# Ten state buffers, an earlier GpSimd inflow, later products with D and earlier SiLU gates in a two-direction Mamba decoder layer

## The reference, cut to what matters

```python
xz = jnp.einsum('bld,ed->ble', x, Win)
u, z = jnp.split(xz, 2, axis=-1)
uc = _silu(causal_conv4(u))                    # 512 channels
x_dbl = jnp.einsum('bld,ed->ble', uc, Wx)      # 16 ranks, 32 B rows, 32 C rows
dt = softplus(x_dbl[..., :16] @ Wdt.T + bdt)
A = -exp(Alog)                                 # 512 channels x 32 states
h = exp(dt_t * A) * h + (dt_t * u_t) * B_t     # step over 100 tokens
y = einsum('bdn,bn->bd', h, C_t) + uc * Dp
y = y * _silu(z)
out = einsum('bld,ed->ble', y, Wout)
```

## Time and profile before

| | before |
|---|---|
| median of 3 runs | 1164.34 us (1163.25 to 1166.03) |
| profiled execution, its time | 1168.91 us |
| its span in the trace | 1166.8 us |
| PE busy | 1009.4 us (87%) |
| DVE busy | 808.7 us (69%) |
| ACT busy | 756.4 us (65%) |
| POOL busy | 628.8 us (54%) |
| granted TensorE clock, mean | 0.945 |

### The profile page before, as it was taken

How to read it: one execution, slowest core, us unless ns; L and a number is a source line. 1 busy time by engine, 2 the same in 40 slices (tenths; PEclk the granted TensorE clock), 3 DMA queues, 4 the chain that set the end, 5 groups by cost and what they waited for, 6 DMA issues and landing times.

```text
span 1166.8 us, 16801 instructions
## 1 busy us (share of the span) xinstructions
PE 1009.4 (87%) x5808; PEld 691.1 (59%) x5808; DVE 808.7 (69%) x954; ACT 756.4 (65%) x1727; POOL 628.8 (54%) x389
## 2 busy tenths in 40 slices
PE   5795788988889898888988898898989799799995
PEld 3342554555555455554555566677767556699994
DVE  6786999998999989999899945756666721111110
ACT  4789998888989888898888911455565532133331
POOL 2000899898999989899899933421210005022222
PEclk9897799999999999999999999979998979899998
DMA  5001333343444433343444401430000006689994
GB/s 180 8 7 36 87 108 108 98 109 91 116 110 96 117 96 103 107 106 105 102 109 106 107 22 62 131 93 15 14 2 2 2 0 220 216 257 321 300 319 113
DMA packets 91119, 125.45 MB, mean 108 GB/s; under 512 B 11641, under 2 KB 84490, under 8 KB 91018
## 3 DMA queue, kind: packets, MB, share of 16 engines
q1 hardware_dynamic: 87130, 120.04, 35.8%
q0 software_dynamic: 3904, 4.33, 2.0%
HBM read 115.93 MB, written 9.23 MB: 107 GB/s over the span
## 4 chain that ended last, share of the span: by engine, by line
PE 37%; DVE 26%; issue 12%; DMA 11%; POOL 6%; ACT 6%; DVEq 0%; POOLq 0%; ACTq 0%
DVE states L1681 14%; PE ps L1186 12%; DMA sums<-y_tile,x_tile 10%; DVE states L1659 5%; PE ps L1077 4%; PE ps L1067 3%; PE ps L1167 3%; POOL states L663 3%; PE ps L1279 3%; PE ps L1291 2%; POOL states L672 2%; PE ps L1084 2%; DVE neg_max L1762 2%; PE ps L1177 2%; ACT probs L989 2%
## 5 line engine op out<-in xcount | busy, mean ns | idle before, releaser
L672 POOL TENSOR_TENSOR states<-states,c_row 128x800 f32<-128x800 f32 x255 | 473.9, 1889 | 131.8 <-DVE states L1681 131.8
L1186 PE MATMUL ps<-states,ident 128*128 128x400 f32 x1024 | 370.7, 506 | 0.0
L1186 PEld LDWEIGHTS ps<-states,ident 128*128 128x128 f32 x1024 | 188.2, 193 | 119.2 <-issue 7.5
L1681 DVE TENSOR_TENSOR_SCAN states<-ps,states 128x800 f32<-128x800 f32 x128 | 230.5, 1801 | 12.4 <-POOL states L663 12.4
L1681 DVE TENSOR_TENSOR_SCAN states<-sb_decay,ps 128x800 f32<-128x800 f32 x128 | 231.4, 1808 | 10.7 <-ACT sb_decay L901 10.6
L893 ACT ACTIVATE xT<-xn_tok,xT 100x256 f32<-100x256 f32 x512 | 216.4, 493 | 14.8 <-PE ps L1167 14.7
L901 ACT ACTIVATE ps<-dt,neg_a 128x396 f32<-128x396 f32 x256 | 141.8, 586 | 57.9 <-DVE states L1681 56.9
L1167 PE MATMUL ps<-ident,xT 100*128 100x100 f32 x1024 | 113.9, 255 | 73.1 <-DVE states L1681 70.9
L1167 PEld LDWEIGHTS ps<-ident,xT 100*128 100x128 f32 x1024 | 97.9, 144 | 131.6 <-issue 127.0
L901 ACT ACTIVATE sb_decay<-dt,neg_a 128x396 f32<-128x396 f32 x256 | 144.4, 612 | 2.4 <-DVE states L1681 2.4
L1048 ACT ACTIVATE hid_tile<-ps,w_tile 128x128 f32<-128x128 f32 x160 | 45.6, 368 | 105.0 <-PE ps L1490 105.0
(11 more groups left out here) (225 smaller groups left out, 1270.1 us busy)
## 6 DMA issues: line engine op xcount, KB each, us to landing
c_row<-rows SPq DMA_DIRECT2D x256, 200.0 KB, 3.1
w_tile<-in_w SPq DMA_DIRECT2D x40, 1024.0 KB, 7.9
b_row<-rows SPq DMA_DIRECT2D x32, 200.0 KB, 3.1
ctx<-in_ctxT SPq DMA_DIRECT2D x8, 361.0 KB, 4.1
rows_by_slot<-blank_rows SPq DMA_DIRECT2D x1, 2660.0 KB, 11.5
x_tile<-rows_by_slot SPq DMA_DIRECT2D x20, 133.0 KB, 3.7
win<-in_winT SPq DMA_DIRECT2D x2, 1024.0 KB, 10.8
w_shared<-in_w SPq DMA_DIRECT2D x2, 1024.0 KB, 6.6
```

The costliest lines, as they stand in the source:

```text
L672: nc.gpsimd.tensor_tensor(st, st, c_row[i % C_SLOTS][:].unsqueeze(1).broadcast_to([P, CP, TQ]), ALU.mult).then_inc(product_ready, 1)
L1186: mm = nc.tensor.matmul(ps[:, j, 0:TQ], ident[:], states[i % RING][:, j * TQ:(j + 1) * TQ], start=False, stop=(i % N == N - 1), skip_group ...
L1681: nc.vector.tensor_tensor_scan(st, rates, inflows, 0.0, ALU.mult, ALU.add).then_inc(scan_done, 1)
```

## The change

What it does:

- `RING` goes from 8 to 10 state buffers (4 x 800 bytes per partition each).
- GpSimd issues `pool_inflow` three rounds ahead of its step (POOL_AHEAD) instead of two.
- The products with D no longer open a segment. The first `sum_state` of a segment starts the accumulation (and waits for `y_gated` there), and the products with D join it behind the sum of state 12 (`add_skip`, SKIP_AT = 12).
- On TensorE the row of B for the next VectorE inflow is issued in the round of the inflow before it (so the one of step 9 mod 8 moves from round 7 to round 5), and in a segment's start the transposes of step 8 are issued in round 6, ahead of the sum of state 1, instead of round 7.
- The z tiles of channels 0 and 1 of direction 0 are computed right behind `x` and go from PSUM through SiLU straight into `gate`, while SiLU's table is still in from the convolution; direction 0's `x` rows are copied ahead of the last two SiLUs of the convolution. The other z tiles come ahead of their dt tile. The SiLU of the other six gate tiles stands right behind the last dt tile, and the scaled tokens of step 2 stand behind the decays of step 1.

The diff, cut:

```diff
@@ -55,12 +55,12 @@
-RING = 8
+RING = 10
 SEG = DIRS * Q * (CT // CP)
 STEPS = SEG * N
 C_SLOTS, B_SLOTS = 4, 1
 POOL_EVERY, POOL_AT = 8, 7
-SUM_LAG, GATE_AT = 5, 5
+SUM_LAG, GATE_AT, SKIP_AT = 5, 5, 12
 TURNED_AT, TURN_EVERY = 0, 2
 TURN_DTU_AT, COPY_DTU_AT = (9, 15), (11, 17)
 SCALED_SLOTS, SB_DECAYS = 2, 2
@@ -130,6 +132,17 @@
 
 POOL_STEPS, DVE_STEPS, TURNED_STEPS = counts_of(on_pool), counts_of(on_dve), counts_of(turned_in)
 BANK_STEPS = [i + 1 - TURNED_STEPS[i] for i in range(STEPS)]
+
+
+def products_of(d):
+
+    early = [("z", c) for c in range(CT) if d == 0 and c < SILU_EARLY]
+    rest = []
+    for c in range(CT):
+        if ("z", c) not in early:
+            rest.append(("z", c))
+        rest.append(("dt", c))
+    return early + rest
 
 
 def bank_jobs():
@@ -150,9 +163,8 @@
     for d in range(DIRS):
         for q in range(Q):
             jobs.append((("x", d, q), "a"))
-        for c in range(CT):
-            channel("dt", d, c)
-            channel("z", d, c)
+        for name, c in products_of(d):
+            channel(name, d, c)
     for d in range(DIRS):
         for h in range(B // 2):
             jobs.append((("mix", d, h), "a"))
@@ -674,8 +687,8 @@
 
             pool.wait_ge(dtu_ready, DIRS * CT)
             for i in range(STEPS - 1):
-                if on_pool(i + 2) and i + 2 < STEPS:
-                    pool_inflow(i + 2)
+                if on_pool(i + POOL_AHEAD) and i + POOL_AHEAD < STEPS:
+                    pool_inflow(i + POOL_AHEAD)
                 state_times_c(i)
 
             last = STEPS - 1
@@ -849,21 +862,24 @@
                 steps += 2
                 nc.scalar.activation(dt_sb[d][:, c, :], e, ACT.Ln, bias=1.0).then_inc(log_ready, 1)
 
-            def copy_gates(d, c):
+            def copy_gates(d, c, func=ACT.Copy):
                 for q in range(Q):
-                    copy_out(("z", d, c, q), gate[d][:, c, chunk(q)], bank(("z", d, c, q))[:, 0:TQ])
-
-            def silu_gates(d):
-                job_copied(act, ("z", d, CT - 1, Q - 1))
-                for c in range(CT):
-                    nc.scalar.activation(gate[d][:, c, :], gate[d][:, c, :], ACT.Silu).then_inc(gate_ready, 1)
+                    copy_out(("z", d, c, q), gate[d][:, c, chunk(q)], bank(("z", d, c, q))[:, 0:TQ], func)
+
+            def silu_gates(d, c):
+                job_copied(act, ("z", d, c, Q - 1))
+                nc.scalar.activation(gate[d][:, c, :], gate[d][:, c, :], ACT.Silu).then_inc(gate_ready, 1)
 
             steps = 0
-            for g in range(DIRS * CT):
+            units = DIRS * CT
+            for g in range(units):
                 copy_u(*divmod(g, CT))
-                if g >= 1:
+                if 1 <= g < units - 1:
                     silu_u(*divmod(g - 1, CT))
-            silu_u(DIRS - 1, CT - 1)
+            copy_x(0)
+            for g in range(units - 2, units):
+                silu_u(*divmod(g, CT))
+                copy_gates(0, g - (units - SILU_EARLY), ACT.Silu)
             nc.scalar.preload_act_table_set("natural_log_exp_and_others")
 
             for d in range(DIRS):
@@ -871,10 +887,17 @@
                 nc.scalar.activation(neg_a[d][:], neg_a[d][:], ACT.Exp).then_inc(rate_ready, 1)
             act.wait_ge(conv_ready, DIRS * CT)
             for d in range(DIRS):
-                copy_x(d)
+                if d:
+                    copy_x(d)
+                for name, c in products_of(d):
+                    if name == "dt":
+                        softplus_parts(d, c)
+                    elif d or c >= SILU_EARLY:
+                        copy_gates(d, c)
+            for d in range(DIRS):
                 for c in range(CT):
-                    softplus_parts(d, c)
-                    copy_gates(d, c)
+                    if d or c >= SILU_EARLY:
+                        silu_gates(d, c)
 
             def copy_dtu(s, h, at=DTU_BANK):
                 act.wait_ge(dtu_turned, 2 * s + h + 1)
@@ -922,14 +945,12 @@
                 copy_dtu(0, h, FIRST_DTU_BANKS[h])
             act.wait_ge(b_tok_ready, 1)
             scale_tokens(0)
-            scale_tokens(2)
-            for d in range(DIRS):
-                silu_gates(d)
             act.wait_ge(neg_a_ready, DIRS)
             act.wait_ge(dt_ready, DIRS * CT)
             sb_decays(0)
             act.wait_ge(decay_zeroed, 1)
             bank_decays(1)
+            scale_tokens(2)
             sb_decays(2)
             for i in range(1, STEPS, 2):
                 if i > 1:
@@ -1111,15 +1132,17 @@
                 for q in range(Q):
                     product(("x", d, q), 2 * N + R, TQ, [
                         (wx_sb[d][:, c, :], u_sb[d][:, c, chunk(q)]) for c in range(CT)])
-                pe.wait_ge(rank_ready, Q * (d + 1))
-                for c in range(CT):
+                for name, c in products_of(d):
+                    if name == "z":
+                        in_product("z", 1, d, c)
+                        continue
+                    pe.wait_ge(rank_ready, Q * (d + 1))
                     for q in range(Q):
                         product(("dt", d, c, q), P, TQ, [(wdt_sb[d][:, tile(c)], rank_sb[:, chunk(q)])])
-                    in_product("z", 1, d, c)
 
 
             pe.wait_ge(consts, CONSTS)
-            for key, _ in JOBS[JOB[("z", DIRS - 1, CT - 1, Q - 1)] - 7:][:8]:
+            for key, _ in JOBS[LAST_OF_MIXER - 7:][:8]:
                 job_copied(pe, key)
             pe.wait_ge(parts_ready, DIRS)
             pe.wait_ge(diag_ready, DIRS)
@@ -1168,23 +1191,24 @@
                                                  scaled[turn % SCALED_SLOTS][:, b, tile(j)], ident[0:L, 0:L])
                 mm.then_inc(inflow_turned, 1)
 
-            def open_segment(s):
+            def add_skip(s):
                 d, q, cp, _ = place(s * N)
-                if s:
-                    pe.wait_ge(y_gated, s)
                 for j in range(CP):
                     c = cp * CP + j
-                    nc.tensor.matmul(ps[:, j, 0:TQ], diag_d[d][:, c, :], u_sb[d][:, c, chunk(q)], start=True,
+                    nc.tensor.matmul(ps[:, j, 0:TQ], diag_d[d][:, c, :], u_sb[d][:, c, chunk(q)], start=False,
                                      stop=False, skip_group_check=True)
 
             def sum_state(i):
+                s, n = divmod(i, N)
+                if s and n == 0:
+                    pe.wait_ge(y_gated, s)
                 if i < STEPS - 1:
                     pe.wait_ge(product_ready, i + 1)
                 for j in range(CP):
                     if i == STEPS - 1:
                         pe.wait_ge((product_ready, last_half)[j], (STEPS, 1)[j])
                     mm = nc.tensor.matmul(ps[:, j, 0:TQ], ident[:], states[i % RING][:, j * TQ:(j + 1) * TQ],
-                                          start=False, stop=(i % N == N - 1), skip_group_check=True)
+                                          start=(n == 0), stop=(n == N - 1), skip_group_check=True)
                 mm.then_inc(y_summed, 1)
 
             turn_b()
@@ -1192,19 +1216,32 @@
                 turn_dtu(0, h, FIRST_DTU_BANKS[h])
             b_row_bank(1)
             turn_inflow(0)
+            def turned_after(i):
+
+                s, n = divmod(i, N)
+                if s and n == GATE_AT + 1:
+                    return i + 2
+                if s and n == GATE_AT + 2:
+                    return None
+                return i + 1
+
             for i in range(STEPS + SUM_LAG):
-                if i + 2 < STEPS and on_dve(i + 2):
-                    b_row_bank(i + 2)
-                if i + 1 < STEPS and turned_in(i + 1):
-                    turn_inflow(i + 1)
+                if i < STEPS and on_dve(i):
+                    for j in range(i + 1, min(i + POOL_EVERY, STEPS)):
+                        if on_dve(j):
+                            b_row_bank(j)
+                            break
+                ahead = turned_after(i)
+                if ahead is not None and ahead < STEPS and turned_in(ahead):
+                    turn_inflow(ahead)
                 s, n = divmod(i, N)
                 if s + 1 < SEG and n in TURN_DTU_AT:
                     turn_dtu(s + 1, TURN_DTU_AT.index(n))
                 behind = i - SUM_LAG
                 if behind >= 0:
-                    if behind % N == 0:
-                        open_segment(behind // N)
                     sum_state(behind)
+                    if behind % N == SKIP_AT:
+                        add_skip(behind // N)
 
             pe.wait_ge(y_gated, SEG)
             for d in range(DIRS):
@@ -1684,7 +1721,8 @@
                 d, q, cp, _ = place(s * N)
                 pair_of = slice(cp * CP, (cp + 1) * CP)
                 dve.wait_ge(y_summed, (s + 1) * N)
-                dve.wait_ge(gate_ready, d * CT + (cp + 1) * CP)
+                if d * CT + (cp + 1) * CP > SILU_EARLY:
+                    dve.wait_ge(gate_ready, d * CT + (cp + 1) * CP - SILU_EARLY)
```

7 lines of the change are left out of this document (5 added, 2 removed).

## The result

The changed kernel takes 1120.88 us (median of 4 runs, 1118.76 to 1126.22) against 1164.51 before (4 runs); the ratio is 0.964, 95% interval 0.9606 to 0.9674. The forecast was 1124, range 1117 to 1136. The profiled span fell by 46.0 us, from 1166.8 to 1120.8.

What follows compares the result with a forecast made beforehand. No engine bounded the whole kernel; in the scan VectorE stood still 33.8 us, waiting for GpSimd's inflow and TensorE's rows. Scan gain 27.8 plus lead-in 12 gave 40 us: 1164.3 - 40 = 1124, range 1117 to 1136.

Steps and rivals of the forecast that it cites:

- GpSimd's inflow (12.4 us): Scan: VectorE's 12.4 us wait before odd scans, about 0.4 in each of 32 turns, goes with inflow three rounds ahead.
- The boundary (17.9 us to 3.0): Scan's segment boundaries: VectorE's 17.9 us wait for rows of B shrinks to five low-clock stalls of 0.6.
- Ten buffers, at nothing: Scan boundary: two more state buffers costed at nothing, but they let the inflow and boundary terms stand.
- Products with D in round 17, at nothing: Scan: the two matmuls, 1.36 us at full clock, moved to round 17; TensorE needs 4.9 us, VectorE arrives after 6.1.
- First rounds, 0.5 us: Scan's first segment: 0.5 us of stall expected to remain, added beside the boundaries' 3.0.
- About 2 in the first rounds: Scan start: about 2 us counted as removed, on top of 12.4 and 17.9.
- 1.0 us for two engines not in step: Scan: 1.0 us added because VectorE and GpSimd, within 2% of each other, cannot always be in step.
- GpSimd's floor of 533: Scan: 32 x 16.65 us of GpSimd's products and inflows taken as its floor; forecast scan to scan 534.
- Lead-in, 12 us: Before the first scan, read on ScalarE: 11.9 us saved, taken as 12; bounds 4.5 and 13.
- The last item (4.5): Lead-in, last dt tile to decays: covered TensorE wait 1.28, two fewer SiLU tiles 1.55, four scalings moved 1.65; together 4.5.
- The rivals: Boundary keeps wait: 1132, 12%; lead-in gives a third: 1132, 10%; early inflow stays late: 1136, 5%; GpSimd stretches: 1172, 3%.
- the slower one: Scan: GpSimd's products stretch beside a gapless VectorE; at 2.02 us each, 1172 us; sign: products over 1.95 us; 3%.

Runs made afterwards that it cites:

- one kernel above: Changed kernel with the six in-place SiLUs and the scalings of step 2 back in their old places before the first scan: 1118.34 us, ratio 0.9604.
- the one with the old order: Changed kernel with TensorE's rows of B and transposes of step 8 back in their old rounds: 1131.46 us, ratio 0.9712.
- the last version: Changed kernel with decays of step 3 ahead of step 4's scaled tokens and TensorE's lag shortened in the last 12 rounds: 1119.21 us, ratio 0.9606.

## Why the prediction was right, and where its terms were off

- **GpSimd's inflow (12.4 us).** Right: 12.4 to nothing in the trace, and 12.3 back when undone. It was lost as 0.5 us in 25 turns, the seven with a gating being free of it, and not as 0.4 in all 32. The slack of 2.3 us in its loop held.
- **The boundary (17.9 us to 3.0).** Right in kind; the rest was 1.1. Two of my steps were pessimistic: the clock fell behind three gatings, not five, and the waits then were 0.33, 0.29 and 0.53, not 0.6. A low boundary had cost 1.7 us in the kernel before (71.2 against 69.5 from gating to gating) and costs 0.4 now (66.9 against 66.5). The windows of the changed kernel behind its second and its seventh gating:

```profile
249.90:253.90 4.00, 4.00 (x14) 2.43 (x15) 4.00 (x3) 3.45 (x9) 4.00 (x3) 0.62 0.38 103
...
583.10:587.10 4.00, 4.00 (x14) 2.56 (x15) 4.00 (x3) 3.45 (x9) 4.00 (x3) 0.61 0.43 109
```

- **Ten buffers, at nothing, as what lets the others stand.** Right: 11.5 us of the scan when taken from the changed kernel, nothing that shows when given to the kernel before. The parts do not add up: taken away one at a time, the four parts of the scan lengthen it by 12.5, 11.5, 12.4 and 7.9, 44.3 in all, where together they gave 29.8. At a boundary each is worth its full price only with the others in place.
- **Products with D in round 17, at nothing.** Right: gatings are 66.47 to 66.9 us apart, as VectorE's work alone is.
- **First rounds, 0.5 us.** Too low: 1.14 + 1.19 and some tenths. ScalarE writes the decays of step 3 behind the tokens of step 4, and TensorE runs its first sums at a low clock (0.51 from 100 to 120 us). I had thought of TensorE's half only.
- **"About 2 in the first rounds", as removed.** A misreading that the sum got away with. The first rounds' waits of the kernel before (0.36 at 130.05 and 1.61 at 133.5) are already inside the 12.4 and 17.9. What was left over is the price that a wait has beyond its row: VectorE's instructions overlap by 0.08 us when none waits, and lose that at a wait. In the kernel before 33 waits, 30.3 us by their rows, lengthened the distances between starts by 32.5. It left together with the waits.
- **1.0 us for two engines not in step, and GpSimd's floor of 533.** Not there. VectorE's train fits to the hundredth between boundaries. The 533 was no floor from scan to scan, since GpSimd's products may trail: its last whole one starts 2.1 us behind the last scan, and one kernel above had a scan of 529.9.
- **Lead-in, 12 us.** It was 13.6 (13.4 without the scatter at its start), and its first half was right: the last Ln ended 7.56 us earlier (97.82 to 90.26), forecast 7.4. Two small errors cancel there: 1.9 instead of 1.2 ahead of the first dt tile, 5.7 instead of 6.2 behind it. The last item (4.5) measured 6.0 (17.82 to 11.78 us from the end of the last Ln to the first scan). Its three terms came: the wait of 1.28 went, two SiLUs fewer gave 1.6, the scalings 1.6. But the wait went because of the order of z and dt, not because SiLUs covered it, and the scalings' 1.6 was given back before the fourth scan. Left out was the last gate copy, 0.8, that no longer stands behind the last Ln, and 0.8 at the copies of tokens, most of it the short waits beside the one I took.
- **The rivals.** None showed. Of the slower one, 105 of GpSimd's 255 products had records longer than the 1.95 us that I had named as a sign (median 1.887 before, 1.928 after), but in the second profile of the same kernel none had (median 1.890), and the distance between starts was 1.845 in all three. The sign was badly chosen; the chain did not stretch.

The sum was 40 us; the median moved 43.6, the profiled span 46.0, of which 2.6 is scatter. The scan gave 2.0 more than its term and the lead-in 1.6 more.

The clock rule of the Trainium skill ("TensorE: Matmul & The Clock Gate", Part 1) says that an idle array runs at half speed until it has been busy again. I had counted every pause as idle and so got seven low boundaries; the page does not say that a pause of 1.62 us is enough, and the traces agree with my reading behind some gatings only. Seven times 0.6 would have been further from the measured 1.1 than my five times.

## What to carry to other kernels

Before buffers are added, ask which wait they end: ten buffers gave nothing that shows while program order held the row behind the gating, and 8 us by the median, 11.5 in the profiled scan, once it did not. Where one instruction must wait for another engine, put everything that others need soon ahead of it, and leave behind it only what has slack, counted at the low clock too. An item moved out of the way at the start of a pipeline is only won if the pipeline does not ask for it a few steps on: read the gain at the end of the loop, not at its first instruction.

## What the runs showed of the hardware that was not expected

**The same pause, two clocks.** TensorE pauses 1.62 to 1.63 us at every boundary of every kernel here. Behind it the granted clock, as the mean of 4 us, was 0.50 to 0.63 in three of seven cases in the changed kernel, five in the kernel before and in the one with the old order, six with eight buffers, seven with D at the opening and none with the inflow two rounds ahead, and 1.00 in the others. In two profiles of the changed kernel it was three each time, but not the same three, so the program alone does not settle it. A boundary therefore needs its margin at 1.2 GHz. What decides a case stays open.

**Two SBUF operands beside GpSimd.** The last step's second half is multiplied by VectorE with both operands in SBUF, 128 x 400, while GpSimd works on its own. The changed kernel's rows, then those of the kernel before:

```profile
636.38 3.52 DVE L1741 TENSOR_TENSOR states<-states,c_row 128x400 f32<-128x400 f32 x1
638.39 1.08 POOL L698 TENSOR_TENSOR states<-states,c_row 128x400 f32<-128x400 f32 x1
...
679.80 2.14 DVE L1703 TENSOR_TENSOR states<-states,c_row 128x400 f32<-128x400 f32 x1
681.46 1.37 POOL L685 TENSOR_TENSOR states<-states,c_row 128x400 f32<-128x400 f32 x1
```

VectorE's instruction took 2.11 to 2.15 us in four kernels (the one before, that with ten buffers, the changed one with the inflow two rounds ahead, and the last version) and 3.5 to 4.0 in all others. An operation of VectorE of twice the size with one operand in PSUM takes 0.96. That agrees with the page "SBUF — State Buffer" of the Trainium skill (section on the two sides), by which a VectorE operation with two SBUF inputs and a GpSimd operation that reads SBUF exclude each other.

What sets 2.1 or 3.5 can be read from the traces together. In all fourteen VectorE's instruction ends 0.42 to 0.44 us behind the end of one of GpSimd's. In the four short cases it starts 0.16 to 0.24 us into GpSimd's last whole product and ends behind that one, and GpSimd's own half product takes 1.37 to 1.40 us. In the ten long cases it starts one product earlier, and ends only behind the half product (1.02 to 1.09 us), so GpSimd's instructions in a row all went first. About 0.43 us, half of the 0.88 between starts for twice the size, is then its own work (an estimate), and the rest is waiting.

The scans, with one operand in PSUM, showed nothing of the kind: 1.79 to 1.82 us in all kernels. Here the wait cost nothing, since TensorE's eight sums run without a gap to 642.93 and set the last gating.
